# Attention scores from float32r high and low parts in four row groups, instead of bf16 thirds stacked over 72 rows

## The reference, cut to what matters

```python
def _L0_attn_ref(x, wq, bq, wk, bk, wv, bv, wo, bo):
    q = jnp.einsum('bsd,hde->bhse', x, wq) + bq      # (8, 16, 512, 8)
    k = jnp.einsum('bsd,hde->bhse', x, wk) + bk
    v = jnp.einsum('bsd,hde->bhse', x, wv) + bv
    scale = 1.0 / jnp.sqrt(jnp.asarray(q.shape[-1], q.dtype))
    scores = jax.nn.softmax(jnp.einsum('bhse,bhte->bhst', q, k) * scale, axis=-1)
    att = jnp.einsum('bhst,bhte->bhse', scores, v)
    ...
h = _layernorm(x, axis=-1) * (1 + ca) + sa
x = x + ga * _L0_attn_ref(h, ...)
```

## Time and profile before

| | before |
|---|---|
| median of 3 runs | 1170.81 us (1170.74 to 1175.88) |
| the profiled execution | 1174.08 us, span 1172.4 us |
| mean granted clock of TensorE | 0.901 |
| TensorE (matmul) busy | 981.7 us, 84%, 6249 matmuls |
| VectorE busy | 766.4 us, 65% |
| ScalarE busy | 579.6 us, 49% |
| GpSimd busy | 444.3 us, 38% |
| data moved by DMA | 90.11 MB |

### The profile page before, as it was taken

The page is one execution under the profiler, slowest core; times in us unless marked ns, Lnnn a source line. Parts: engine busy times, 40 slices in busy tenths (PEclk is TensorE's granted clock), DMA queues, the critical chain, the costliest instruction groups (busy, mean ns, idle before and its releaser), DMA issues.

```text
span 1172.4 us, 21238 instructions
## 1 busy us (share of the span) xinstructions
PE 981.7 (84%) x6249; PEld 616.0 (53%) x6249; DVE 766.4 (65%) x1912; ACT 579.6 (49%) x1225; POOL 444.3 (38%) x625
## 2 busy tenths in 40 slices
PE   4699999999899999994198999999996539999764
PEld 3133333333233333332197888889885439999621
DVE  3668787878687878896188756665665336656333
ACT  1057676767576767771023533552453116666421
POOL 4030414131222222121324565665534336666532
PEclk9569999999899999996599999999998559999876
DMA  4432323232232324510600010100101012222232
GB/s 141 140 120 75 132 72 131 74 128 76 100 105 97 106 96 108 186 49 10 277 19 19 20 31 27 31 26 22 33 8 48 18 33 68 65 68 68 82 92 75
DMA packets 55645, 90.11 MB, mean 77 GB/s; under 512 B 9393, under 2 KB 40539, under 8 KB 54902
## 3 DMA queue, kind: packets, MB, share of 16 engines
q1 hardware_dynamic: 45942, 58.68, 17.5%
q0 software_dynamic: 9600, 30.24, 7.2%
HBM read 49.62 MB, written 39.30 MB: 76 GB/s over the span
## 4 chain that ended last, share of the span: by engine, by line
PE 34%; DVE 6%; DMA 3%; issue 3%; POOL 3%; ACT 3%; SPq 0%; DVEq 0%; ACTq 0%; POOLq 0%
PE a L2030 6%; PE tb L1860 5%; PE a L1852 4%; PE a L1870 4%; PE b_ L2039 3%; PE c L1826 2%; PE a L2039 2%; PE b_ L1826 2%; DMA weights<-back_dram 1%; DMA xg<-tokens_dram,row_of 1%; PE b_ L1922 1%; PE b_ L1821 1%; ACT L1418 1%; PE b_ L1914 1%; POOL rows_dram L1303 1%
## 5 line engine op out<-in xcount | busy, mean ns | idle before, releaser
L630 DVE TENSOR_REDUCE nmax<-ps_s 128x1 f32<-128x512 f32 x512 | 324.8, 683 | 87.7 <-PE ps_s L795 86.5
L524 ACT ACTIVATE p_ring<-ps_t 128x512 f32<-128x512 f32 x512 | 287.2, 597 | 141.6 <-PE ps_t L806 138.1
L817 PE MATMUL ps_av<-p_ring,v_ext 128*32 128x512 f32 x1024 | 138.8, 615 | 0.0
L795 PE MATMUL ps_s<-weights 72*128 72x512 bf16 x256 | 108.3, 427 | 19.5 <-DMA weights<-q_parts_dram 15.6
L1466 ACT ACTIVATE weights<-a,wtile 128x128 f32<-128x128 f32 x288 | 82.3, 368 | 49.5 <-PE a L2030 49.5
L1330 POOL DMA_INDIRECT back_dram<-weights,target x72 | 84.0, 1167 | 57.8 <-DVE weights L1783 51.9
L806 PE MATMUL ps_t<-weights 75*128 75x512 bf16 x256 | 102.0, 398 | 2.6 <-ACT p_ring L524 1.5
L806 PE MATMUL ps_t<-q_stack,k_stack 75*128 75x512 bf16 x256 | 96.7, 382 | 3.9 <-ACT p_ring L524 2.0
L795 PE MATMUL ps_s<-k_stack,q_stack 72*128 72x512 bf16 x256 | 98.1, 383 | 1.3 <-DVE nmax L630 1.3
L1374 ACT ACTIVATE hid<-a 128x512 f32<-128x512 f32 x64 | 38.2, 597 | 112.5 <-PE a L1852 112.3
L1303 POOL DMA_INDIRECT rows_dram<-hrow,slot x64 | 63.2, 988 | 64.5 <-DVE slot L1690 46.1
(11 more groups left out here) (286 smaller groups left out, 1681.2 us busy)
## 6 DMA issues: line engine op xcount, KB each, us to landing
rows_dram<-wmod POOLq DMA_DIRECT2D x8, 2145.0 KB
q_parts_dram<-q_parts SPq DMA_DIRECT2D x40, 128.0 KB, 2.4
xt<-rows_dram SPq DMA_DIRECT2D x72, 65.0 KB, 1.8
weights<-k_parts_dram SPq DMA_DIRECT2D x16, 288.0 KB
weights<-q_parts_dram SPq DMA_DIRECT2D x16, 288.0 KB
k_stack<-k_parts_dram SPq DMA_DIRECT2D x16, 288.0 KB
q_stack<-q_parts_dram SPq DMA_DIRECT2D x16, 288.0 KB
wall<-in_wall SPq DMA_DIRECT2D x1, 4112.0 KB, 20.7
```

What stands on the lines that cost most here:

```text
L524: nc.scalar.activation(probs[:, u % RING, :], ps_t[u % TBANKS][:], ACT.Exp, scale=HD ** -0.5).then_inc(exp_done, 1)
L630: nc.vector.tensor_reduce(nmax[:, js, n:n + 1], ps_s[u % SBANKS][:], AX.X, ALU.max, negate=True).then_inc(max_done, 1)
L795: nc.tensor.matmul(ps_s[u % SBANKS][:], q_stack[par][0:STACK, h, quarter(t)], k_stack[par][0:STACK, h, :], start=True, stop=True).then_inc ...
L817: last = nc.tensor.matmul(ps_av[32 * g:32 * (g + 1), :], v_ext[par][:, t, HG * j + g, :], probs[:, (HG * k + g) % RING, :], start=(t == 0) ...
```

## The change

q and k are split into two float32r parts (a float32 whose low mantissa bits are rounded away), and three products are kept: first by first, first by second, second by first. So a stack has 3 x 8 = 24 rows per head, and 26 for `score_t` with the two parts of the maximum. Each of the four heads of a group has 32 partitions of its own (`GROUP`), which puts its matmuls in one of TensorE's four row groups. `score` takes the heads of a group in another order than `score_t` (`head_of_score`), so that by units the row groups are 2, 0, 3, 1, 0, 2, 1, 3. The stacks have tiles of their own for both parities.

ScalarE writes the first part as float32r, VectorE the second directly. GpSimd's `split` is gone, its `maxima` has two operations instead of four, and it fills both k stacks with ones at the start. SyncE saves three slots for k and three for q, loads eight pieces of 24 partitions (one per row group, all head groups at once), first k's and then q's, and moves the maxima with two DMAs. The first score of a batch waits for all eight loads.

```diff
-PARTS = 3
-TERMS = PARTS * PARTS
-STACK = TERMS * HD
+PARTS = 2
+K_SLOTS = (0, 0, 1)
+Q_SLOTS = (0, 1, 0)
+SLOTS = len(K_SLOTS)
+STACK = SLOTS * HD
 MROW = STACK
+GROUP = P // HG
...
+def head_of_score(v):
+    return (v + 2) % HG
...
-        even = [weights0[:, i].bitcast(BF16).rearrange("p (h t) -> p h t", h=H) for i in range(2)]
-        q_stack = [even[0], sb("q_stack1", [P, H, T], BF16)[:]]
-        k_stack = [even[1], sb("k_stack1", [P, H, T], BF16)[:]]
+        q_stack = [sb(f"q_stack{i}", [P, NG, T]) for i in range(2)]
+        k_stack = [sb(f"k_stack{i}", [P, NG, T]) for i in range(2)]
...
-            for i in range(2):
-                sp.dma_start(k_stack[i][MROW:MROW + PARTS], ones[:]).then_inc(ones_in, 16)
...
-                sp.dma_start(q_stack[par][MROW:MROW + PARTS, HG * j:HG * (j + 1), :],
-                             m_rows[:, j, :]).then_inc(m_in[j], 16)
+                for c in range(PARTS):
+                    sp.dma_start(q_stack[par][MROW + c:P:GROUP, j, :],
+                                 m_rows[HG * NT * c:HG * NT * (c + 1), j, :]).then_inc(m_in[j], 16)
...
-            def load_stacks(j, par):
-
-                n = HG * T
-                sp.dma_start(k_stack[par][0:STACK, HG * j:HG * (j + 1), :],
-                             window(scratch["k"], n * j, [[H * T, PARTS * HD], [0, PARTS], [1, n]])
-                             ).then_inc(stack_in[j], 16)
-                sp.dma_start(q_stack[par][0:STACK, HG * j:HG * (j + 1), :],
-                             window(scratch["q"], n * j, [[H * T, PARTS * HD], [HD * H * T, PARTS], [1, n]])
-                             ).then_inc(stack_in[j], 16)
...
+            def load_stacks(stack, dram, par):
+
+                for g in range(HG):
+                    sp.dma_start(stack[par][GROUP * g:GROUP * g + STACK, :, :],
+                                 window(dram, T * g, [[H * T, STACK], [HG * T, NG], [1, T]])).then_inc(stack_in, 16)
...
-                nc.gpsimd.tensor_copy(parts[:, 1, :], rest[:]).then_inc(second, 1)
-                pool.wait_ge(second, bb + 1)
-                nc.gpsimd.tensor_tensor(parts[:, 2, :], rest[:], parts[:, 1, :], ALU.subtract).then_inc(third, 1)
...
-                    dve.wait_ge(third, nxt)
-                    nc.vector.scalar_tensor_tensor(rst[:], bank[:], bias[:], parts[:, 0, :], ALU.add, ALU.subtract
-                                                   ).then_inc(ready, 1)
+                    nc.vector.scalar_tensor_tensor(parts[:, 1, :], bank[:], bias[:], parts[:, 0, :].bitcast(F32),
+                                                   ALU.add, ALU.subtract).then_inc(second, 1)
...
-                if v == 0:
-                    pe.wait_ge(stack_in[js], 32 * (bs + 1))
+                if js == 0 and v == 0:
+                    pe.wait_ge(stack_in, 16 * 2 * HG * (bs + 1))
...
-                h, t = HG * js + v % HG, v // HG
-                nc.tensor.matmul(ps_s[u % SBANKS][:], q_stack[par][0:STACK, h, quarter(t)], k_stack[par][0:STACK, h, :],
-                                 start=True, stop=True).then_inc(s_filled, 1)
+                first, t = GROUP * head_of_score(v), v // HG
+                rows_ = slice(first, first + STACK)
+                nc.tensor.matmul(ps_s[u % SBANKS][:], q_stack[par][rows_, js, quarter(t)].bitcast(F32R),
+                                 k_stack[par][rows_, js, :].bitcast(F32R), start=True, stop=True).then_inc(s_filled, 1)
...
-                h = HG * j + g
-                nc.tensor.matmul(ps_t[u % TBANKS][:], k_stack[par][0:STACK + PARTS, h, quarter(t)],
-                                 q_stack[par][0:STACK + PARTS, h, :], start=True, stop=True).then_inc(t_filled, 1)
+                rows_ = slice(GROUP * g, GROUP * g + STACK + PARTS)
+                nc.tensor.matmul(ps_t[u % TBANKS][:], k_stack[par][rows_, j, quarter(t)].bitcast(F32R),
+                                 q_stack[par][rows_, j, :].bitcast(F32R), start=True, stop=True).then_inc(t_filled, 1)
```

More of the change, by code:

```diff
@@ L260, in program_attention @@
         k_saved = sem("k_saved")
-        stack_in = [sem(f"stack_in{j}") for j in range(NG)]
+        stack_in = sem("stack_in")
         s_filled = sem("s_filled")
@@ L393, in iteration @@
                         settle(sp)
[L394 removed]
+                    if not it.here:
+                        sp.wait_ge(consts, 3)
+                    sp.wait_ge(k_saved, 16 * SLOTS * (nxt + 1))
                     settle(sp)
[L396 removed]
+                    load_stacks(k_stack, scratch["k"], 1 - par)
+                    sp.wait_ge(q_saved, 16 * SLOTS * (nxt + 1))
                     settle(sp)
[L398 to L399 removed]
+                    load_stacks(q_stack, scratch["q"], 1 - par)
                 if not it.here and it.after:
@@ L431, in _ @@
         def _(pool):
-            nc.gpsimd.memset(ones[:], 1.0).then_inc(consts, 1)
             nc.gpsimd.memset(half[:], -0.5).then_inc(consts, 1)
             for i in range(2):
+                nc.gpsimd.memset(k_stack[i][:], 1.0).then_inc(consts, 1)
+            for i in range(2):
                 nc.gpsimd.memset(v_ext[i][:], 0.0).then_inc(consts, 1)
-                pool.wait_ge(consts, 3 + 2 * i)
+                pool.wait_ge(consts, 4 + 2 * i)
                 nc.gpsimd.memset(v_ext[i][:, :, :, HD:HD + 1], 1.0).then_inc(consts, 1)
-            def split(rest, rest_ready, parts, second, third, saved, slots, bb):
-                pool.wait_ge(rest_ready, bb + 1)
-                pool.wait_ge(saved, 16 * slots * bb)
-                settle(pool)
-                nc.gpsimd.tensor_copy(parts[:, 1, :], rest[:]).then_inc(second, 1)
-                pool.wait_ge(second, bb + 1)
-                nc.gpsimd.tensor_tensor(parts[:, 2, :], rest[:], parts[:, 1, :], ALU.subtract).then_inc(third, 1)
             def maxima(bb, j):
-                done = 3 * (NG * bb + j)
                 pool.wait_ge(max_done, UNITS * bb + HG * NT * (j + 1))
@@ L486, in iteration @@
                     ).then_inc(emptied, 16)
-                if it.after:
-                    split(k_rest, k_rest_ready, k_parts, k2_ready, k3_ready, k_saved, PARTS, nxt)
-                    split(q_rest, q_rest_ready, q_parts, q2_ready, q3_ready, q_saved, QSLOTS, nxt)
                 if it.before:
@@ L673, in rest @@
                 def rest(which):
-                    bank, bias, parts, rst, first, ready, third = {
-                        "q": (bank_a, bq, q_parts, q_rest, q1_ready, q_rest_ready, q3_ready),
-                        "k": (bank_b, bk, k_parts, k_rest, k1_ready, k_rest_ready, k3_ready)}[which]
+                    bank, bias, parts, first, second = {
+                        "q": (bank_a, bq, q_parts, q1_ready, q2_ready),
+                        "k": (bank_b, bk, k_parts, k1_ready, k2_ready)}[which]
                     dve.wait_ge(first, nxt + 1)
-                    dve.wait_ge(third, nxt)
-                    nc.vector.scalar_tensor_tensor(rst[:], bank[:], bias[:], parts[:, 0, :], ALU.add, ALU.subtract
-                                                   ).then_inc(ready, 1)
+                    nc.vector.scalar_tensor_tensor(parts[:, 1, :], bank[:], bias[:], parts[:, 0, :].bitcast(F32),
+                                                   ALU.add, ALU.subtract).then_inc(second, 1)
                 def values():
```

96 lines of the change are left out of this document (33 added, 63 removed).

## The result

Four runs of the changed kernel took 1240.14 to 1265.4 us, median 1251.58; the kernel before, on the same chip, 1173.35. The ratio is 1.0634 (95% interval 1.0529 to 1.0739): slower by 6%, where the forecast was 1.2%. It is taken from the fast runs, so the slow one of 1265.4 is not in it.

What follows compares the result with a forecast made beforehand. TensorE was taken to set attention's pace, ScalarE's ping-pong right behind. 1174.1 - 8 - 15 - 3 + 40 = 1188.1, or 1185 us against the 1170.8 median; own range 1170 to 1230, wide range 1140 to 1300.

Steps and rivals of the forecast that it cites:

- own range: Total time of the main forecast: 1170 to 1230 us, chance 0.42.
- Clock, +40: Attention: narrow scores let TensorE's clock fall to 0.50 in every batch, 140 us at 0.29, +40 us, bounds 0 and +158.
- a third of 450 us: Attention: share of time at clock 0.50, from units 4 to 9 until behind the projections, taken as 140 us.
- Float32r, taken as one pass like bf16: Score matmuls: a float32r matmul of 512 columns taken as one pass, 0.22 us, like bf16.
- a matmul of 0.6 us: Score matmuls: the forecast counts as wrong if a float32r matmul lasts 0.6 us at clock 1.00.
- Overlap, -15 and -3: Scores in different row groups start 0.11 apart: -15 us over seven batches, -3 in two stretches at clock 0.50.
- drains: Rival: every change of shape in attention drains the array, 0.16 x 34 a batch, total 1183 with clock held; chance 0.10.
- the 0.9 a batch: Attention: cost of some 17 changes between row groups and whole array, 0.05 us each, per batch.
- the 0.09 that the prediction held against the rule: Ahead of a weighing: the seen cost of a change of shape, where the skill's drain rule would give 0.16.
- Start, -8: Kernel start: earlier saves and loads bring the first score from 39.00 to 31.5, -8 us, bounds -5 and -10.
- DMA, 0: Attention: fewer saves, eight smaller loads all awaited by a batch's first score, 0 us, bound +2 us a batch.
- The rest of the kernel, 0: Behind attention, which ends at about 532 us: the change was said to touch only attention, no term given.

Runs made afterwards that it cites:

- before_rows128: The kernel before with score and score_t matmuls over all 128 rows (rows 75 to 127 zero) instead of 72 and 75: median 1175.86 us.
- full_rows: The changed kernel with every score and score_t matmul over all 128 rows instead of 24 and 26, scores wrong: median 1179.33 us.
- bf16_groups: The changed kernel with stacks, parts and maxima in bfloat16 instead of float32r, same four row groups, scores less exact: median 1213.93 us.
- rows64: The changed kernel with 64 rows per score and score_t matmul instead of 24 and 26, two side by side, scores wrong: median 1163.66 us.
- halves6: The kernel before with split_first, six bf16 products instead of nine, 64 rows per matmul, two heads in each array half: median 1147.7 us.
- split_first: The kernel before with GpSimd's first split of k and q ahead of the clearing of the fill rows: median 1162.73 us.
- same_group: The changed kernel with the scores' head order shifted by two, so score and score_t of a unit share a row group: median 1445.0 us.

## Why the prediction was wrong in size and right in direction

The measured 1251.58 lies above the prediction's own range of 1170 to 1230 and inside the wide one of 1140 to 1300. The direction came from the right mechanism; the size came out too small by two terms, the clock's and that of float32r, which was put at nothing.

**Clock, +40: the mechanism was right, the size half.** It forecast 140 us at 0.50 at 0.29 each; it was 251.6 more than before, at 0.31 to 0.33 each 78 to 83 us. The price was nearly right. The step that failed is "a third of 450 us": it put the fall into units 4 to 9 of a batch and trusted the projections to bring the clock back. By the clock's records it did rise at unit 11, right behind the projection of q, in batches 0, 2, 3 and 5, and the low time ahead of unit 11 was 110 us. But the clock fell again later in the batch (at units 26 and 52 of batch 0, 50 of batch 1, 28 of batches 2 and 4): 168 us were low from unit 11 on, 47 of them in the last batch. In batch 1 (129.5 to 202.4) 45.6 of 72.9 us were low.

**Float32r, taken as one pass like bf16: missing term of +24.** At the same 128 rows, from before_rows128 to full_rows, the stage went from 461.9 to 486.2; the loads and GpSimd's work differ between these two as well, but from 77 to 485 us TensorE of full_rows waited for no load and 2.2 us for GpSimd (6.0 in before_rows128). That is 3.0 us a batch, where 44 of 128 score matmuls last 0.45 us or more. In row groups, from bf16_groups to the changed kernel, the difference is 24.1 us, and 125 of 128 are long. The prediction's own test (a matmul of 0.6 us) was set too coarsely to catch 0.50. The Trainium skill (TensorE: Matmul & The Clock Gate, Weight-path perf modes) says that the fast weight load is on when 128 weights are loaded and the type is not FP32. The rows don't show it for float32r: a weight load of 128 columns takes 0.22 us on the mean here, 0.19 in full_rows at a high clock, against 0.10 for bf16 before. Whether that makes the matmul longer no run shows.

```profile
L761 PEld LDWEIGHTS ps_s<-k_stack,q_stack 24*128 24x128 f32 x512 | 83.9, 220 | 197.6 <-DVE nmax L596 109.4 <-issue 71.8 <-DMA q_stack<-q_parts_dram 11.9
```

**Overlap, -15 and -3: right in size, and drains right as a rival.** As the remainder, 82.4 less 78 to 83 and less 24, it brought 20 to 25 us with the drains taken off, an estimate that hangs on the price of the clock; full_rows against rows64 gives 22, and in bf16 before_rows128 against halves6 8.1, or 16 with 26.4 us more at 0.50 priced at 0.31. The distance was underrated (0.01 against 0.11) and so was the change of shape: 0.05 was taken, and transposes behind a score of a row group start 0.42 behind it, behind one of 128 rows 0.24. That is the rival with a chance of 0.10; it is true, but as one term, not the outcome. (Its sum, 1183, also counts the 0.9 a batch twice that it says it replaces; without that it is 1177.) A new shape starts 0.07 to 0.08 ahead of the modelled end of the last matmul, whether that lasts 0.38, 0.50 or 0.79 (198.88 to 199.60). The Trainium skill's rule on a drain at a change of tiling mode (TensorEngine Tiling (Array Packing), Key Properties) agrees with these rows. It agrees with the 0.31 ahead of a weighing, too: the 0.09 that the prediction held against the rule is what a wait for that point costs.

**Start, -8: it was -4.1.** The first score came at 34.88:

```profile
34.88 0.80 PE L761 MATMUL ps_s<-k_stack,q_stack 24*128 24x512 f32 x3 [11.61 <-DMA q_stack<-q_parts_dram]
```

```profile
16.76 1.92 SPq L350 DMA_DIRECT2D k_parts_dram<-k_parts  x3
18.77 1.90 SPq L350 DMA_DIRECT2D q_parts_dram<-q_parts  x3
21.23 3.33 SPq L356 DMA_DIRECT2D k_stack<-k_parts_dram  x4
24.67 3.16 SPq L356 DMA_DIRECT2D q_stack<-q_parts_dram  x4
```

The loads went out 0.7 late (21.23 for 20.5, the last at about 24.67 + 3/4 of 3.16 = 27.0 for 26.3), and from the last issue to the score it took 7.8 where 5.2 had been taken: the last of eight loads landed later than the second of four had. GpSimd's clearings cost nothing (its norm starts at 8.54, at 8.51 before). And the gain is not one of the new stacks: split_first, with the old ones, brought the first score to 32.21.

**DMA, 0: right.** In the whole trace the scores waited 11.6 us for a stack, and that is the 11.61 of the first one. **The rest of the kernel, 0: it was -7.2.** The last batch took 69.9 us instead of 51.5, and VectorE does rounds of the top-k beside it. Of 32 rounds 20 were left behind the stage, 22 before; at 2.16 us a round that is at most 4.3 us. The rest stays open: with a last batch of 50 to 55 us what follows took 634.1 to 640.3 in the kernels here, with one of about 70 us or more 633.1 to 635.8, and no run was made for it.

## What to carry to other kernels

A busy TensorE can still lose its clock: look at the granted clock of a stretch before and after narrowing a matmul. Here rows of zeros cost nothing in a matmul's duration (0.38 us at 72 and at 128 rows in bf16) and held the clock; their clearing pays only where its engine waits anyway. Row groups paid with two groups of 64 rows in bf16 (halves6); with four of 24 and 26 the kernel was slower, with four of 32 about as fast as before. Each change between row groups and the whole array waited until 0.07 to 0.08 us ahead of the modelled end of the last matmul.

## What the runs showed of the hardware that was not expected

- Zeros count: 26.4 us at 0.50 became 1.9 with 53 rows of zeros (20.5 became 6.9 with the same start), 284.5 became 127.1 with six to eight further rows, zeros most of them.
- Overlap and clock go together: the same matmuls with two side by side kept the clock at 0.50 for 707.2 us, with up to four for 278.0.
- In same_group two scores of neighbouring units start within 0.01 us, by the trace ahead of the score_t that stands between them in the program (153.08, 153.67).
- A float32r matmul of 512 columns lasts 0.39 to 0.40 us right behind another or right behind a pair, and 0.48 to 0.50 behind other work or behind a wait, at 24 and 64 rows as at 128. The bf16 one lasts 0.37 to 0.39 in all these places.
- Four row groups start within 0.01 us. In a plain group of float32r this brought nothing (3.12 us against 3.10), in bf16 0.19 us (2.91): as these rows read, the longer matmul stands in the chain between two exponentials and takes the gain back.
